# The last four pairs through all experts, and a new cut of the other 28 into chunks

## The chip, the cores and the metric

One core of one Trainium2 chip. The metric is the device time of one execution in microseconds (us), the median of the runs shown.

## The reference

Inputs: `x` (64, 128, 256), a context (64, 128, 192), and weights. Per sequence:

```
x = x + cross_attention(layernorm(x), context)     # 16 heads of 64, 128 queries, 128 keys, then a projection
x = x + experts(layernorm(x))                      # 8 experts, top 2 per token
experts: probs = softmax(t @ gate.T); w, idx = top_k(probs, 2)
         y_e = silu(t @ expert_w[e].T + expert_b[e])          # e = 0..7, 256 -> 256
         out = (sum over the 2 picked of w * y_idx) @ combine_w.T
```

Everything is in float32. The expert biases are eight times as large as drawn.

## The kernel before, in words

**Precision.** Each operand of a matmul is split in a high part (`fp32r`) and the rest, and a product is three matmuls: high by high, high by low, low by high (`three`). ScalarE writes the high part out of PSUM (`split_hi`, L703), VectorE subtracts it for the low one (`split_lo`, L845). SiLU is made of a tanh on ScalarE (L757) and `(1 + tanh) * y` on VectorE (L910); the half is in the routing weights.

**Pairs and slots.** Two sequences (256 tokens) are a pair, 32 in all. A pair's attention takes eight slots, one for two heads; slot `s` belongs to pair `s // 8`, `u = s % 8`. In each slot every engine goes through its own list in program order. TensorE: transpose the probabilities of the slot before, early jobs, queries and keys three slots ahead, scores of the next slot, mid jobs, attend, project, late jobs. GpSimd: split the attended values, divide the probabilities by their sums (`normalise_probs`, L1139, once a slot), then scatters (L1158) and gathers (L1170). SyncE issues the direct transfers, in order, among them the copies `k_s<-qk_s` that each slot's scores wait for.

**Jobs of a slot.** They share three PSUM banks (`gen_ps`). Of the attention: values (slots 1, 2, 5, 6), transposes of the normalised input (3) and of the attention's normalised output (4, `turn_x1`, into `x1T`), gate logits (5), and rank (7): for each token the row that it gets in the table of its expert.

**Experts.** Pairs are gathered in chunks, `CHUNKS = (8, 8, 7, 6, 3)`. Tokens are scattered by expert into `sorted_x` in HBM (four indirect transfers a pair, two pairs later). After the last pair of a chunk VectorE lists its blocks (`list_blocks`, L994 to L1020, in slot 7), and SyncE clears the rows behind each expert's last token (`clear_after`, L370: eight transfers whose addresses are values read from memory). A chunk of `n` pairs has `4n + 7` blocks of 128 rows: 163 in all. A block is one slot: load its rows (L408), its expert's split weights (L422, 512 KB) and bias, two transposes (L617), seven matmuls of 256 columns, tanh, SiLU, store into `sorted_y` (L429). The weights have a ring of three.

**Mixes.** For each pair: four gathers from `sorted_y`, four multiplications by the routing weights on ScalarE (`weigh`, L787), eight transposes that add the two picks (`turn_sum`, L584) in the next slot, split, and `combine`, 12 matmuls, one slot on; VectorE adds the residual (L916) and SyncE stores the output (L483). The chain of one pair goes through one buffer, `mT_s`.

**Order.** `Plan` writes out which slot runs which block (`turn`), gather and mix. `room` gives how many gathers a slot may issue: in the attention 0 in slots 0 to 3 and 1 in slots 4 to 7; behind it 2, and later 4. Attention ends with slot 255. Blocks in slots up to 255: 123 of the 163; mixes up to slot 255: 16 of 32. The rest, 40 blocks and 16 mixes, runs behind the attention; the last slot is 310.

Of the kernel before, what the change touches and what calls it, by code (L numbers as in the profile page):

```python
# [22 lines left out]
CHUNKS = (8, 8, 7, 6, 3)  # L23
# [15 lines left out]
KINDS = ("value", "turn_x", "turn_x1", "gate", "rank", "turn_block", "expert", "turn_mixed", "combine")  # L39
# [11 lines left out]
class Plan:  # L51


    def __init__(self, pairs):
        assert sum(CHUNKS) == pairs
# [7 lines left out]
        for c, end in enumerate(self.ends):  # L63
# [5 lines left out]
            for m in range(end - CHUNKS[c], end):  # L69
# [7 lines left out]
                free += 1  # L77
        self.last = max(max(self.turn) + 4, max(self.mix) + 4)
        self.jobs_at, order = {}, []
        for s in range(-SLOTS, self.last + 1):  # L80
            i, u = s // SLOTS, s % SLOTS
            early, mid, late = [], [], []
            for kind, k, off in ATTENTION_JOBS.get(u, []):
                if 0 <= i + off < pairs:
                    mid.append((kind, (i + off) * per(kind) + k))
# [28 lines left out]
def xattn_moe_kernel(nc, x, ctxT, wq, wkv, wkv_rest, wproj, bproj, gateT, expertT, expert_b, combineT, out):  # L114
# [21 lines left out]
    with ExitStack() as stack:  # L136
# [19 lines left out]
        ones_s = sb("ones_s", [P, P], F32R)  # L156
        minus_half = sb("minus_half", [P, 2])
# [23 lines left out]
        before_f = sb("before_f", [P, P])[:, :]  # L181
# [30 lines left out]
        y_row = carve(4 * max(CHUNKS), 1)  # L212

# [18 lines left out]
        row_f = sb("row_f", [P, pairs, 4])  # L232
# [70 lines left out]
        rstd_done = [sem(f"rstd_done{n}") for n in (1, 2)]  # L303

# [37 lines left out]
        def _(sp):  # L342
# [87 lines left out]

            load_x(0)
# [10 lines left out]
            for s, i, u in slots():  # L442
# [47 lines left out]
        def _(pe):  # L490
# [56 lines left out]
            def project(j, p):  # L547
# [5 lines left out]
                if j == 0 and p == HEAD_PAIRS - 1:  # L553
                    pe.wait_ge(bias_in, 16)
                    pe.wait_ge(const_r, 2)
# [40 lines left out]
            def gate(j, bank):  # L596
# [3 lines left out]
                for t in range(2):  # L600
                    mm = products(bank[:, t * 2 * E:(t + 1) * 2 * E], [
                        (part[:, a, t * P:(t + 1) * P], wgate[:, a, :]) for a in range(2) for part in x1T])
                return mm

            def rank(j, bank):
                pe.wait_ge(hot_done, j + 1)
                if j == 0:
                    pe.wait_ge(const_r, 2)
# [32 lines left out]

            def general(s, position):
                for kind, n in plan.jobs_at[s, position]:
# [19 lines left out]
                    elif kind == "turn_mixed":  # L663
                        pe.wait_ge(weighted, n + 1)
                        mm = turn_sum(got[n % 2], bank)
                    else:
# [4 lines left out]
            for s, i, u in slots():  # L671
# [23 lines left out]
                general(s, "late")  # L695


        @block.scalar
        def _(act):
# [59 lines left out]
            def general(s, position):  # L759
                for kind, n in plan.jobs_at[s, position]:  # L760
# [9 lines left out]
                    elif kind == "turn_x1":  # L770
                        wait(act, made["gate"], n)
                        to = x1T[0][:, :, :].rearrange("p a n -> p (a n)")
                        split_hi(made[kind], n + 1, [(to, bank[:, :])], hi_of[kind])
# [27 lines left out]
            for s, i, u in slots():  # L801
# [11 lines left out]
                if s - 2 in plan.turn:  # L813
                    tanh(plan.turn[s - 2][2])
                general(s, "early")
# [9 lines left out]
                if s in plan.mix:  # L825
# [15 lines left out]
        def _(dve):  # L841
# [101 lines left out]
            def route_top(j):  # L943
# [10 lines left out]
                if j == 0:  # L954
# [4 lines left out]
                                       ALU.is_equal))  # L959
                both = picks.rearrange("p (t k) e -> p t k e", k=2)  # L960
# [11 lines left out]

            def chosen_of(j):
                n = j - (plan.ends[plan.chunk_of[j]] - CHUNKS[plan.chunk_of[j]])
# [47 lines left out]
            def general(s, position):  # L1022
                for kind, n in plan.jobs_at[s, position]:
# [6 lines left out]
                    elif kind in ("turn_x", "turn_x1", "turn_mixed"):  # L1030
                        hi, lo = (y[:, :, :].rearrange("p a n -> p (a n)") for y in
                                  {"turn_x": xT[n % 2], "turn_x1": x1T, "turn_mixed": mT_s}[kind])
                        split_lo(hi_of[kind], n + 1, [(lo, bank[:, :], hi)], drained[kind])
# [22 lines left out]
            for s, i, u in slots():  # L1056
# [7 lines left out]
                if u == 2 and before:  # L1064
                    add_residual(i - 1)
                general(s, "early")
# [25 lines left out]
                if u == 3 and before:  # L1092
                    wait(dve, made["turn_x1"], i - 1)
                    wait(dve, scattered[(i - 1) % 2], 64 * ((i - 1) // 2))
# [7 lines left out]
                if u == 0 and exists(i - 2):  # L1102
                    route_weights(i - 2)
                if i == -1 and u == 4:
# [12 lines left out]
        def _(pool):  # L1117
# [68 lines left out]
            pool.memset(ones_s[:, :].bitcast(F32), 1.0).then_inc(const_r, 1)  # L1186
            pool.memset(before_f, 1.0).then_inc(const_c, 1)
# [5 lines left out]
            for s, i, u in slots():  # L1193
# [11 lines left out]
                if u < 4 and exists(i - 2):  # L1205
# [46 lines left out]
```

## Time and profile before

| | |
|---|---|
| runs | 1726.19 us median of three (1721.33 to 2524.45) |
| the profiled execution | 1724.26 us, span 1722.5 us, mean granted TensorE clock 0.957 |
| busy: TensorE, VectorE, ScalarE, GpSimd | 90%, 72%, 62%, 53% of the span |
| moved by DMA | 303.81 MB, 176 GB/s over the span |

Busy shares are of the span of the profiled execution. In tables of stretches PEclk is the granted clock of TensorE, 1.00 being 2.4 GHz and 0.50 being 1.2 GHz; a value between them is a mean over both levels.

### The profile page before, as it was taken

Reading aid. Unit: us, or ns where it says so; the run is one execution under the profiler, and the core shown is the slowest. Engines: PE = TensorE matmul, PEld = TensorE weight load, DVE = VectorE, ACT = ScalarE, POOL = GpSimd, SP = SyncE. Lnnn points to the kernel's source line nnn. Section 1 sums busy time; section 2 is a strip of 40 time slices with the busy share of each in tenths; the row PEclk is TensorE's granted clock in tenths of the full one; section 3 lists DMA queues with packets and bytes.
Section 4 is the critical chain, followed back from the end, with each engine's and each line's share of the span. In section 5 each row is a group of like instructions: output and inputs, shape, how many; then the busy total and the mean of one; then the engine's idle time right before and its main releaser. Section 6 shows DMA issues by size and latency. Waiting matters only on the chain.

```text
span 1722.5 us, 39484 instructions
## 1 busy us (share of the span) xinstructions
PE 1547.0 (90%) x11835; PEld 1473.5 (86%) x11835; DVE 1236.4 (72%) x3090; ACT 1063.0 (62%) x2904; POOL 915.1 (53%) x1214
## 2 busy tenths in 40 slices
PE   4889999999999999989999999899999989865664
PEld 4789999898999999988999999889999989854554
DVE  6667878887888888877787878877888778642222
ACT  5656666665666766666676666666667656632232
POOL 4645555654555455665555556555555566542132
PEclk9999999999999999999999999999999999977577
DMA  6733333333677775335777775357777645777784
GB/s 226 248 102 93 90 93 99 91 92 102 182 215 219 212 216 156 104 106 165 224 224 223 221 219 150 103 171 223 221 223 226 176 118 171 219 234 234 240 277 149
DMA packets 187211, 303.81 MB, mean 176 GB/s; under 512 B 24725, under 2 KB 119162, under 8 KB 186490
## 3 DMA queue, kind: packets, MB, share of 16 engines
q1 hardware_dynamic: 174714, 267.71, 52.7%
q0 software_dynamic: 12288, 33.57, 5.9%
q8 instruction: 99, 1.62, 0.4%
q14 instruction: 110, 0.90, 0.2%
HBM read 164.06 MB, written 70.01 MB: 136 GB/s over the span
## 4 chain that ended last, share of the span: by engine, by line
PE 61%; DVE 11%; issue 8%; POOL 6%; ACT 5%; SPq 5%; DMA 3%; POOLq 0%; ACTq 0%; DVEq 0%
PE gen_ps L493 18%; PE qk_ps L493 13%; PE proj_ps L493 8%; PE s_ps L493 7%; PE o_ps L493 7%; PE pT_ps L534 5%; POOL sorted_x L1158 1%; PE gen_ps L617 1%; PE gen_ps L584 1%; POOL o_s_lo L1150 1%; ACT v_s_hi L703 1%; DVE stats L861 1%; DVE sums L894 1%; POOL rstd L1134 1%; ACT stage L703 1%
## 5 line engine op out<-in xcount | busy, mean ns | idle before, releaser
L730 ACT ACTIVATE stage<-s_ps,neg_max 128x128 f32<-128x128 f32 x1024 | 293.0, 371 | 126.8 <-DVE neg_max L887 114.4
L1148 POOL CAST o_s_hi<-stage 128x256 fp32r<-128x256 f32 x256 | 102.1, 399 | 474.7 <-ACT stage L703 473.1
L1139 POOL TENSOR_TENSOR stage<-stage,inv_sums 128x512 f32<-128x512 f32 x256 | 266.2, 1040 | 20.5 <-DVE inv_sums L896 20.5
L493 PE MATMUL s_ps<-k_s,qk_s 128*128 128x256 f32 x1536 | 227.4, 284 | 13.9 <-DMA k_s<-qk_s 13.3
L703 ACT CAST pT_s_hi<-pT_ps 128x512 fp32r<-128x512 f32 x256 | 151.0, 590 | 129.2 <-PE pT_ps L534 121.0
L894 DVE TENSOR_REDUCE sums<-stage 128x4 f32<-128x512 f32 x256 | 174.9, 683 | 73.3 <-ACT stage L730 68.5
L493 PEld LDWEIGHTS s_ps<-k_s,qk_s 128*128 128x128 f32 x1536 | 201.5, 191 | 15.5 <-DMA k_s<-qk_s 14.4
L845 DVE TENSOR_TENSOR qk_s<-qk_ps,qk_s 128x512 fp32r<-128x512 f32 x256 | 175.7, 686 | 44.2 <-ACT qk_s L703 43.7
L845 DVE TENSOR_TENSOR pT_s_lo<-pT_ps,pT_s_hi 128x512 fp32r<-128x512 f32 x256 | 172.0, 672 | 46.6 <-ACT pT_s_hi L703 43.8
L1170 POOL DMA_INDIRECT stage<-sorted_y,y_row_of x128 | 126.3, 987 | 141.5 <-issue 68.9
L1150 POOL TENSOR_TENSOR o_s_lo<-stage,o_s_hi 128x256 fp32r<-128x256 f32 x256 | 188.1, 735 | 21.1
L703 ACT COPY stage<-o_ps 64x256 f32<-64x256 f32 x512 | 188.4, 368 | 3.6 <-POOL o_s_lo L1150 0.6
L703 ACT CAST v_s_hi<-gen_ps 128x512 fp32r<-128x512 f32 x128 | 75.1, 587 | 182.6 <-PE gen_ps L493 178.3
L887 DVE TENSOR_REDUCE neg_max<-s_ps 128x4 f32<-128x512 f32 x256 | 174.4, 681 | 10.7 <-PE s_ps L493 10.7
L493 PE MATMUL qk_ps<-xT_hi,wq_s_hi 128*128 128x256 f32 x512 | 166.9, 326 | 15.6 <-DVE wkvr_s_lo L856 9.3
L493 PE MATMUL o_ps<-pT_s_hi,v_s_hi 128*128 128x256 f32 x512 | 156.1, 305 | 24.5 <-DVE pT_s_lo L845 22.7
L845 DVE TENSOR_TENSOR xbT_lo<-gen_ps,xbT_hi 128x256 fp32r<-128x256 f32 x163 | 69.1, 424 | 138.4 <-ACT xbT_hi L703 117.6
L703 ACT CAST qk_s<-qk_ps 128x512 fp32r<-128x512 f32 x256 | 152.4, 595 | 25.0 <-PE qk_ps L493 19.9
L493 PE MATMUL gen_ps<-w_block,xbT_hi 128*128 128x256 f32 x652 | 140.4, 309 | 28.9 <-DMA w_block<-expert_table 12.2
L493 PE MATMUL proj_ps<-wproj_s_hi,o_s_hi 128*128 128x256 f32 x512 | 149.8, 293 | 15.8 <-POOL o_s_lo L1150 15.1
L534 PE MATMUL pT_ps<-ident,stage 128*128 128x128 f32 x1024 | 156.9, 276 | 1.6 <-POOL stage L1139 1.0
L1158 POOL DMA_INDIRECT sorted_x<-xn,row_of x128 | 135.1, 1056 | 23.8 <-issue 23.5
(169 smaller groups left out, 4815.9 us busy)
## 6 DMA issues: line engine op xcount, KB each, us to landing
w_block<-expert_table SPq DMA_DIRECT2D x163, 512.0 KB
k_s<-qk_s SPq DMA_DIRECT2D x512, 128.0 KB
stage<-sorted_x SPq DMA_DIRECT2D x163, 128.0 KB
sorted_y<-stage SPq DMA_DIRECT2D x163, 128.0 KB
x_raw<-in_x SPq DMA_DIRECT2D x32, 256.0 KB
c_raw<-in_ctxT SPq DMA_DIRECT2D x32, 256.0 KB
stage<-in_x SPq DMA_DIRECT2D x32, 256.0 KB
x_kept<-x SPq DMA_DIRECT2D x32, 256.0 KB
```

What stands on the lines that cost most here:

```text
L493: mm = pe.matmul(out_ap, l, r, start=start and n == 0, stop=stop and n == len(terms) - 1, skip_group_check=skip)
L534: mm = pe.transpose(pT_ps[:, k * P:(k + 1) * P], probs[p % 2][:, k, :], ident[:, :])
L703: last = act.copy(to, of)
L730: last = act.activation(probs[p % 2][:, k, :], s_ps[:, k * P:(k + 1) * P], ACT.Exp, bias=neg_max[p % 2][:, k:k + 1])
L845: last = dve.tensor_tensor(lo, of, hi.bitcast(F32), ALU.subtract)
L887: dve.tensor_reduce(neg_max[p % 2][:, :], s_ps[:, :].rearrange("p (k n) -> p k n", k=4), AX_X, ALU.max, negate=True).then_inc(max_done, 1)
L894: dve.tensor_reduce(sums[p % 2][:, :], probs[p % 2][:, :, :], AX_X, ALU.add).then_inc(sums_done, 1)
L1139: pool.tensor_tensor(probs[b][:, :, :], probs[b][:, :, :], inv_sums[b][:, :].unsqueeze(2).broadcast_to([P, 4, P]), ALU.mult).then_inc(prob ...
L1148: pool.tensor_copy(hi[:, :, :], o_full).then_inc(o_hi, 1)
L1150: pool.tensor_tensor(lo[:, :, :], o_full, hi[:, :, :].bitcast(F32), ALU.subtract).then_inc(o_lo, 1)
L1158: pool.indirect_dma_start(out=sorted_x, out_offset=bass.IndirectOffsetOnAxis(ap=row_of[:, j % 4, k:k + 1], axis=0), in_=xn2[j % 2][:, k // ...
L1170: pool.indirect_dma_start(out=got[m % 2][:, k, :], out_offset=None, in_=sorted_y[c], in_offset=bass.IndirectOffsetOnAxis(ap=y_row_of[:, m, ...
```

## The change

Pairs 28 to 31 leave the sorted path. They have no rank, no scatter and no gather. When their gate is done (`dense_weights`), VectorE turns the two picks and weights of each token into eight weights, six of them zero. Behind the attention SyncE loads the split weights of all eight experts (four transfers of 1 MB, pieces of 1 KB) over the attention's own weights `wq_s` and `wkv0_s`, and the biases over `wkvr_s` (`load_all_experts`, issued at slot 254). A dense job is one token tile (128 tokens) by two experts: seven matmuls of 512 columns, a tanh of 512, `(1 + tanh) * y` of 512, and two additions of 256 columns into the tile's sum, each scaled by that expert's weight. Eight jobs a pair, 32 in all, three a slot in slots 258 to 267 and two in slot 268. They use the four PSUM banks of the attention (`s_ps`, `pT_ps`, `o_ps`, `qk_ps`). A dense pair's mix is four transposes of that sum, split, and the same `combine`.

The other 28 pairs are cut `(8, 8, 6, 4, 2)`: 39, 39, 31, 23 and 15 blocks, 147 in all. Up to slot 255 there are 143 blocks and 23 mixes; four blocks and nine mixes come behind. The lists and clears of all five chunks fall in the attention (before: four). `room` now gives two gathers in slots 4 to 7, so that up to two pairs are mixed in eight slots, in slots 7 and 1. The last slot is 280.

Small moves: `row_f` and `before_f` go into other buffers, and a constant `first_two` (ones in two rows) takes the place of `ones_s` beside the bias of all experts.

```diff
-CHUNKS = (8, 8, 7, 6, 3)
+CHUNKS = (8, 8, 6, 4, 2)
+SPARSE = sum(CHUNKS)
+DENSE_JOBS = 8
+DENSE_BANKS = 4
+DENSE_PER_SLOT = 3
...
+        self.dense = {}
+        at = SLOTS * pairs + 2
+        for n in range(DENSE_JOBS * (pairs - SPARSE)):
+            m = SPARSE + n // DENSE_JOBS
+            if n % DENSE_JOBS == 0:
+                at = max(at, SLOTS * (m + 2))
+            while len(self.dense.get(at, [])) >= DENSE_PER_SLOT:
+                at += 1
+            self.dense.setdefault(at, []).append(n)
+            if n % DENSE_JOBS == DENSE_JOBS - 1:
+                self.mix[max(at + 2, max(self.mix) + 2)] = m
...
-            return 0 if u < 4 else 1
-        return 4 if i > pairs + 1 else 2
+            return 0 if u < 4 else 2
+        return 4 if s >= SLOTS * pairs + 2 else 2
...
+            def load_all_experts():
+                sp.wait_ge(qk_made, pairs * HEAD_PAIRS)
+                sp.wait_ge(made["value"], 4 * pairs)
+                rows = expert_table[0:E * P, :].rearrange("(e p) c -> p e c", p=P)
+                for part in range(2):
+                    for a in range(2):
+                        to = w_all[part][a].bitcast(F32).rearrange("p (e c) -> p e c", e=E)
+                        at = (2 * part + a) * C
+                        sp.dma_start(to, rows[:, :, at:at + C]).then_inc(dense_in, 16)
+                sp.dma_start(b_all[0:2, :].bitcast(F32).rearrange("h (e c) -> h e c", e=E),
+                             bias_table[0:2 * E, :].rearrange("(e h) c -> h e c", h=2)).then_inc(dense_in, 16)
...
+                if s == SLOTS * pairs - 2:
+                    load_all_experts()
...
+            def dense(n):
+                m, t, q = SPARSE + n // DENSE_JOBS, n % DENSE_JOBS // 4, n % 4
...
+                wait(pe, drained["dense"], n - DENSE_BANKS + 1)
+                pe.wait_ge(drained["turn_x1"], m + 1)
+                cols, rows = slice(q * 2 * C, (q + 1) * 2 * C), slice(t * P, (t + 1) * P)
+                terms = []
+                for a in range(2):
+                    terms += three(xT1[m], (w_all[0][a], w_all[1][a]), lambda y: y[:, a, rows], lambda w: w[:, cols])
+                terms.append((first_two[:, :], b_all[:, cols]))
+                products(dense_ps[n % DENSE_BANKS][:, :], terms).then_inc(made["dense"], 1)
...
+            def tanh_all(n):
+                act.wait_ge(made["dense"], n + 1)
+                wait(act, drained["dense"], n - 1)
+                act.activation(th_all[n % 2], dense_ps[n % DENSE_BANKS][:, :], ACT.Tanh, scale=0.5).then_inc(dense_tanh, 1)
...
+            def dense_out(n):
+                dve.wait_ge(dense_tanh, n + 1)
+                wait(dve, dense_added, 2 * (n - 1))
+                dve.scalar_tensor_tensor(out=y_all[n % 2], in0=th_all[n % 2], scalar=1.0,
+                                         in1=dense_ps[n % DENSE_BANKS][:, :],
+                                         op0=ALU.add, op1=ALU.mult).then_inc(drained["dense"], 1)
...
+            def dense_add(n):
+                m, t, q = n // DENSE_JOBS, n % DENSE_JOBS // 4, n % 4
+                dve.wait_ge(drained["dense"], n + 1)
...
+                for h in range(2):
+                    to = acc[m][:, t, :]
+                    y, w = y_all[n % 2][:, h * C:(h + 1) * C], dense_w[:, m, t, 2 * q + h:2 * q + h + 1]
+                    if q + h == 0:
+                        ins = dve.tensor_scalar(to, y, w, None, ALU.mult)
+                    else:
+                        dve.wait_ge(dense_added, 2 * n + h)
+                        ins = dve.scalar_tensor_tensor(out=to, in0=y, scalar=w, in1=to, op0=ALU.mult, op1=ALU.add)
+                    ins.then_inc(dense_added, 1)
```

## Rows read from the trace of the kernel before

**Rows 1.** Stretches (us from the start): busy time and count by engine, PEclk, DMA share, GB/s

```profile
287.20:328.00 40.80, 39.22 (x304) 37.15 (x304) 32.75 (x81) 27.62 (x75) 23.95 (x34) 1.00 0.35 92
504.50:551.00 46.50, 46.45 (x379) 45.35 (x378) 38.14 (x97) 32.20 (x91) 23.97 (x34) 1.00 0.73 216
922.60:972.30 49.70, 49.05 (x399) 47.60 (x398) 39.34 (x99) 34.09 (x96) 28.14 (x39) 1.00 0.75 224
...
1560.00:1686.00 126.00, 78.97 (x431) 69.36 (x431) 34.84 (x76) 39.08 (x100) 27.60 (x29) 0.72 0.84 257
...
1703.00:1708.00 5.00, 3.45 (x17) 3.08 (x15) 0.69 (x1) 2.29 (x5) 3.03 (x4) 0.50 0.30 85
```

**Rows 2.** Timeline of GpSimd, slot 0 of pairs 6, 7, 11, 12, 20, 21; slot 255

```profile
287.22 1.04 POOL L1139 TENSOR_TENSOR stage<-stage,inv_sums 128x512 f32<-128x512 f32 x1
...
328.01 1.04 POOL L1139 TENSOR_TENSOR stage<-stage,inv_sums 128x512 f32<-128x512 f32 x1
...
504.52 1.04 POOL L1139 TENSOR_TENSOR stage<-stage,inv_sums 128x512 f32<-128x512 f32 x1
...
551.02 1.04 POOL L1139 TENSOR_TENSOR stage<-stage,inv_sums 128x512 f32<-128x512 f32 x1
...
922.61 1.04 POOL L1139 TENSOR_TENSOR stage<-stage,inv_sums 128x512 f32<-128x512 f32 x1
...
972.26 1.04 POOL L1139 TENSOR_TENSOR stage<-stage,inv_sums 128x512 f32<-128x512 f32 x1
...
1498.59 1.04 POOL L1139 TENSOR_TENSOR stage<-stage,inv_sums 128x512 f32<-128x512 f32 x1
```

**Rows 3.** The page's part on DMA issues: count, KB each, us to landing

```profile
w_block<-expert_table SPq DMA_DIRECT2D x163, 512.0 KB
...
sorted_x<-zero_rows SPq DMA_DIRECT2D x1, 4992.0 KB, 17.1
```

**Rows 4.** Timeline of GpSimd: slots 7 and 1 without and with list and clear

```profile
323.42 1.04 POOL L1139 TENSOR_TENSOR stage<-stage,inv_sums 128x512 f32<-128x512 f32 x1
...
332.34 1.03 POOL L1139 TENSOR_TENSOR stage<-stage,inv_sums 128x512 f32<-128x512 f32 x1
...
405.36 1.04 POOL L1139 TENSOR_TENSOR stage<-stage,inv_sums 128x512 f32<-128x512 f32 x1
...
419.43 1.04 POOL L1139 TENSOR_TENSOR stage<-stage,inv_sums 128x512 f32<-128x512 f32 x1
```

**Rows 5.** Timeline of SyncE: the clear behind the attention; the store of slot 254

```profile
1547.45 10.93 SPq L370 DMA_DIRECT2D sorted_x<-zero_rows  x8
...
1493.49 0.34 SPq L429 DMA_DIRECT2D sorted_y<-stage  x1
```

**Rows 6.** Timeline of GpSimd, slot 255: what it waits for after a gather

```profile
1497.42 0.40 POOL L1148 CAST o_s_hi<-stage 128x256 fp32r<-128x256 f32 x1 [1.50 <-ACT stage L703]
```

**Rows 7.** Timeline of TensorE: 512 columns at either clock, and a mix's transposes

```profile
555.65 0.40 PE L493 MATMUL gen_ps<-wkv_s_hi,cT_lo 128*128 128x512 f32 x1
555.89 0.40 PE L493 MATMUL gen_ps<-wkv_s_lo,cT_hi 128*128 128x512 f32 x1
...
92.30 0.63 PE L493 MATMUL gen_ps<-wkv_s_hi,cT_lo 128*128 128x512 f32 x1
92.73 0.63 PE L493 MATMUL gen_ps<-wkv_s_lo,cT_hi 128*128 128x512 f32 x1
...
1521.07 1.10 PE L584 MATMUL gen_ps<-ident,stage 128*128 128x128 f32 x8
```

**Rows 8.** Groups by line and shape, 1500 to 1722 us: busy, mean ns, idle before

```profile
L910 DVE SCALAR_TENSOR_TENSOR stage<-stage,gen_ps 128x256 f32<-128x256 f32 x42 | 17.4, 415 | 18.5 <-DMA sorted_y<-stage 17.9 <-issue 0.3 <-ACT stage L757 0.3
...
L916 DVE TENSOR_TENSOR stage<-gen_ps,stage 128x512 f32<-128x512 f32 x16 | 11.0, 685 | 7.9 <-PE gen_ps L493 7.9
L703 ACT CAST mT_s_hi<-gen_ps 128x512 fp32r<-128x512 f32 x16 | 9.4, 587 | 37.9 <-PE gen_ps L584 34.9 <-issue 3.0
```

**Rows 9.** Timeline of VectorE: the last instruction

```profile
1718.82 0.69 DVE L916 TENSOR_TENSOR stage<-gen_ps,stage 128x512 f32<-128x512 f32 x1 [3.02 <-PE gen_ps L493]
```

More of the change, by code:

```diff
@@ L38 @@
 }
-KINDS = ("value", "turn_x", "turn_x1", "gate", "rank", "turn_block", "expert", "turn_mixed", "combine")
+KINDS = ("value", "turn_x", "turn_x1", "gate", "rank", "turn_block", "expert", "turn_mixed", "combine", "dense")
 def per(kind):
@@ L83, in __init__ @@
             for kind, k, off in ATTENTION_JOBS.get(u, []):
-                if 0 <= i + off < pairs:
+                if 0 <= i + off < (SPARSE if kind == "rank" else pairs):
                     mid.append((kind, (i + off) * per(kind) + k))
@@ L212, in xattn_moe_kernel @@
         y_row = carve(4 * max(CHUNKS), 1)
+        row_f = carve(4, pairs)
+        w_all = [[wq_s[part][:, :, :].rearrange("p a n -> p (a n)"), wkv0_s[part][:, :]] for part in range(2)]
+        b_all = wkvr_s[0]
+        over_v = [v_s[part][:, 0, 0:2 * N2].rearrange("p (a n) -> p a n", a=2) for part in range(2)]
+        whole = lambda pair: [y[:, :, :] for y in pair]
+        xT1 = {j: whole(x1T) for j in range(pairs)}
+        xT1.update({pairs - 3: whole(xT[(pairs - 2) % 2]), pairs - 2: whole(xT[(pairs - 1) % 2]), pairs - 1: over_v})
+        th_all = [y.rearrange("p k n -> p (k n)") for y in probs]
+        y_all = [y[:, :, :].rearrange("p t n -> p (t n)") for y in (x_raw, c_raw)]
+        acc = [xn2[SPARSE % 2][:, :, :], xn2[(SPARSE + 1) % 2][:, :, :], xb, x1[:, :, :]]
+        dense_picks = sb("dense_picks", [P, pairs - SPARSE, 4, E])
+        dense_w = sb("dense_w", [P, pairs - SPARSE, 2, E])
         stats = [sb(f"stats{n}", [P, 2, 6]) for n in (1, 2)]
@@ L303, in xattn_moe_kernel @@
         rstd_done = [sem(f"rstd_done{n}") for n in (1, 2)]
+        two_zero = sem("two_zero")
+        dense_in, dense_tanh, dense_added, dense_w_done = (
+            sem(n) for n in ("dense_in", "dense_tanh", "dense_added", "dense_w_done"))
+        dense_ps = [s_ps, pT_ps, o_ps, qk_ps]
         block = stack.enter_context(nc.Block())
@@ L601, in gate @@
                     mm = products(bank[:, t * 2 * E:(t + 1) * 2 * E], [
-                        (part[:, a, t * P:(t + 1) * P], wgate[:, a, :]) for a in range(2) for part in x1T])
+                        (part[:, a, t * P:(t + 1) * P], wgate[:, a, :]) for a in range(2) for part in xT1[j]])
                 return mm
@@ L695, in _ @@
                 general(s, "late")
+                for n in plan.dense.get(s, []):
+                    dense(n)
         @block.scalar
@@ L814, in _ @@
                     tanh(plan.turn[s - 2][2])
+                for n in plan.dense.get(s - 1, []):
+                    tanh_all(n)
                 general(s, "early")
@@ L824, in _ @@
                 general(s, "mid")
-                if s in plan.mix:
+                if plan.mix.get(s, SPARSE) < SPARSE:
                     weigh(plan.mix[s])
@@ L1030, in general @@
                     elif kind in ("turn_x", "turn_x1", "turn_mixed"):
-                        hi, lo = (y[:, :, :].rearrange("p a n -> p (a n)") for y in
-                                  {"turn_x": xT[n % 2], "turn_x1": x1T, "turn_mixed": mT_s}[kind])
-                        split_lo(hi_of[kind], n + 1, [(lo, bank[:, :], hi)], drained[kind])
+                        hi, lo = {"turn_x": xT[n % 2], "turn_x1": xT1.get(n), "turn_mixed": mT_s}[kind]
+                        split_lo(hi_of[kind], n + 1, [(lo[:, :, :], bank[:, :].rearrange("p (a n) -> p a n", a=2), hi[:, :, :])],
+                                 drained[kind])
                     elif kind == "turn_block":
@@ L1065, in _ @@
                     add_residual(i - 1)
+                todo = plan.dense.get(s - 1, [])
+                for k, n in enumerate(todo):
+                    dense_out(n)
+                    if k > 0:
+                        dense_add(n - 1)
+                if todo:
+                    dense_add(todo[-1])
                 general(s, "early")
```

60 lines of the change are left out of this document (50 added, 10 removed).

## The prediction

> **What bounds the kernel now.** I read the table of stretches first [rows 1]. In the attention TensorE is busy for 39.2 of 40.8 us in a pair without blocks, 46.45 of 46.5 with eight blocks, and 49.05 of 49.7 with eight blocks and a mix: there it has next to nothing left, and each block or mix moved in is paid. Behind the attention the reader should see another bound: from 1560 to 1686 us TensorE is busy for 79 of 126 us at a granted clock of 0.72, while the DMA engines are at 0.84 and 257 GB/s. A block brings 512 KB of weights [rows 3], so the tail is paced by transfers.
>
> Then the timeline of GpSimd, where `normalise_probs` marks every slot [rows 2]. The attention ends at 1498.6 us; the span ends at 1722.5. The tail is **224 us** for 40 blocks and 16 mixes. That is what the change attacks.
>
> **Attention: what is moved in.** Pair 6 (no blocks) takes 328.01 - 287.22 = 40.8 us, pair 11 (eight blocks) 46.5, pair 20 (eight blocks, a mix) 49.65 [rows 2]. So a block costs 5.7 / 8 = 0.71 us there and a mix 3.15.
> - 20 more blocks up to slot 255 (143 for 123): 14.3 us.
> - 7 more mixes (23 for 16): 22.0 us. TensorE alone has some 2.4 us in one: eight transposes (1.1) and 12 matmuls of 256 columns at half of the 0.235 us of one of 512 [rows 7]. That is the lower end for a mix. The changed plan puts two of them into slots 7 and 1 of eight; no pair of before does that, so the price of the second is the unknown: between 2.4 us and twice 3.15.
> - One more list and clear. From slot 7 to slot 1 takes 419.43 - 405.36 = 14.1 us with them and 332.34 - 323.42 = 8.9 without [rows 4]: 5.2 us. Two of the clears (slots 216 and 232) now fall where blocks run; they hold SyncE for 10.9 us behind the attention [rows 5], but in the attention weights are issued about two slots, some 12 us, before they are used.
> - The second gather of a slot: GpSimd still idled 1.50 us in slot 255 behind one gather and ahead of the next attended values [rows 6], and a gather is about 1.0 us, 1.2 with its gap. It fits; were it not to, I would pay 0.3 us a slot in 80 slots at most, 24 us. In block slots, which are longer, it has more room. I take 0.
> - Removed: the rank of three pairs and the scatters of two. They lie beside TensorE's work; 0 to 3 us.
>
> The sum is 41.5. Four of the early mixes now run in slots without blocks, where TensorE is not full, and the mix of slot 255 does its work behind the attention. I take **+38 us** (range 30 to 65), so slot 255 comes at 1536.6.
>
> **Tail, start of the dense jobs.** The store of slot 254 was issued 5.1 us before slot 255's mark [rows 5, 2], and the big load follows it. For its time the nearest row is the transfer of 4992 KB in pieces of 1 KB, 17.1 us [rows 3]; 4.1 MB by that is 14 us. With a block's weights in front, it lands about 11 us behind the mark. The weights of the last blocks are issued after it on the same queue, and TensorE wants blocks 143 and 144 before the first dense job. I take 15 us from the mark to the first dense job; 10 to 28 are possible.
>
> **Tail, the dense slots 258 to 268.** TensorE's sum at 2.4 GHz:
> - 32 jobs of seven matmuls, 0.235 us each [rows 7]: 52.6 us.
> - four mixes: 4 x (1.0 + 1.4) = 9.5; three experts and two block transposes: 3.0; `turn_x1` and gate of pair 31: 1.5.
> Together 66.6 us. VectorE's sum: a dense job is one operation of 512 columns (0.685) and two of 256 (0.415 each, and some 0.05 for waiting on its own semaphore) [rows 8], 1.6 us; 32 of them are 51.5. Add 5.5 for the mixes, 2.5 for blocks, 5 for the last pair's normalisation and top 2: 64.5 us. ScalarE has a tanh of 512 (about 0.59, as its cast of 512) a job, 19 us in all. So two engines are nearly full together, with four banks and two buffers between them. I add 3 us for friction: **70 us**.
>
> **Tail, the end.** Mixes 27 to 31 come behind the last dense job and go one by one through `mT_s`: transposes 0.5, high part 0.59, low part 0.69, combine 1.4, handovers 0.25: 3.4 us at 2.4 GHz. At 1.2 GHz a matmul of 512 columns starts every 0.43 us in place of 0.235 [rows 7], which gives 5.1. The end of before ran at either level, 0.50 from 1703 to 1708 us [rows 1]. I take 4.4 x 5 = 22 us, and 3.7 from the last addition to the end of the span (1722.5 - 1718.8) [rows 9]: **26 us**.
>
> The tail is 15 + 70 + 26 = 111 us where it was 224. The span: 1536.6 + 111 = 1647.6; with the 1.8 us that the profiled execution had beside its span, **1649 us**. Against its 1724.26 that is 75 us less, 4.4%. The median of the runs lies 1.9 us above that execution, so nothing is to be corrected.
>
> **The rivals.**
> *A. The dense slots run at 1.2 GHz.* TensorE fell to the lower level in the tail whenever it waited for transfers [rows 1], and here it waits for a load of 4 MB first, then hands every job over to two engines. Price: 32 x 7 x (0.43 - 0.235) = 43.7 us, and some 12 for mixes and blocks: 1705 us, 1.1% faster, no change to speak of. Against it: the jobs are queued densely, 1.6 us each, with four banks ahead, and the attention, which hands over as often, ran at 1.00. Chance 0.12.
> This is where the Trainium skill speaks against the change. Its page "TensorE: Matmul & The Clock Gate", section "A second HAM failure mode: psum-queue depth-cycling", tells of a kernel with matmuls of 512 columns that cycles through PSUM banks and whose engine idled so often between groups that its clock went up and down. By that rule the time would be up to the one of rival A. The trace's attention also cycles through banks and doesn't show it.
>
> *B. VectorE's chain sets the dense slots.* Each addition waits for the one before it, and a job's result for tanh. Were a job to take 2.4 us on that chain, the dense slots would take 25 us more: 1674 us. For it: the two sums are within 3% of each other. Against it: the order puts the next job's product between a job's own steps. Chance 0.10.
>
> *C. Two mixes in eight slots hinder each other in the attention.* If each mix cost twice 3.15 us, that is 22 x 3.15 = 69 us more, 1718 us, no change. Against it: TensorE has 2.4 us of work in one. Chance 0.05.
>
> *D. The dense slots go one job at a time: slower.* If the next job's matmuls start only when the sum of the one before is there, a job takes 7 x 0.43 (the engine would idle, and so be at its lower level), 0.59, 0.685, 0.83 and 0.3 for handovers: 5.4 us, 173 us for 32 in place of 53. That is 1649 + 120 = 1769 us, slower by 2.6%; it is slower than the bound from 5.2 us a job on. Against it: four banks, and buffers for two jobs of tanh and product. Chance 0.03.
>
> *E. The load holds up the blocks behind it.* If the four last blocks each wait for their weights behind 4 MB, the dense jobs start at 30 us, 15 later: 1664 us. For it: before, copies of the attention were late behind the transfer of 4992 KB. Chance 0.10, inside the forecast's range.
>
> **How the numbers follow.** The forecast, 1649 us with 1625 to 1672, has 0.60. The low end is the attention at +30 and the tail at 95; the high end has the load late and a dense job of 1.9 us. B and E hold 0.20, A 0.12, C 0.05, D 0.03. The range of 1622 to 1700 leaves out D, C, half of A and the luck beyond 1622: less than 2 in 10. A change of under 2% can't be told from none; the bound lies at 1691.7 us, so faster has 0.83 (forecast, B, E, and the mild half of A that stays below the bound at 0.03), same 0.14, slower 0.03.
>
> **What would show it.** Slot 255's mark at 1530 to 1545 us; pairs 24 to 30 of 52 to 56 us; a first dense matmul some 15 us later; 32 groups of seven dense matmuls, starting 0.235 us apart, in 65 to 75 us at a granted clock near 1.00, with VectorE busy for nine tenths; a DMA share that falls to little behind the load; GpSimd idle, and no idle time ahead of the attended values that a gather ends. The prediction is wrong if the dense stretch shows PEclk near 0.5, if pairs with two mixes take over 60 us, or if TensorE waits for `dense_in` or block weights for over 15 us.

## The result, and the profile after

The changed kernel takes **1665.37 us**, median of four (1662.45 to 1667.21); the kernel before took 1724.74, median of four beside it. The ratio is **0.9658 [0.9643, 0.9672]**: 3.4% faster. One of the four runs of the kernel before took 2524.45 us, a slow one, which the ratio leaves out. Forecast were 1649 us, in a range of 1622 to 1700. The profiled execution had 1667.21 us and a span of 1665.4.

The page of the changed kernel, its slices and its largest group of transfers. In the slices each digit stands for a fortieth of the span: the busy share, for PEclk the granted clock, in tenths.

```profile
span 1665.4 us, 39339 instructions
PE 1548.1 (93%) x11891; PEld 1475.1 (89%) x11891; DVE 1269.0 (76%) x3134; ACT 1060.3 (64%) x2888; POOL 880.6 (53%) x1184
...
PE   4989999998999999999999999999999998999696
...
PEclk9989999999999999999999999999999999999898
DMA  6743333333577777344677677467776776877621
...
w_block<-expert_table SPq DMA_DIRECT2D x147, 512.0 KB
```

The DMA row now falls to 2 and 1 at the end, where before a stretch of 126 us ran at 0.84 [rows 1], and `w_block` has 147 transfers for 163 [rows 3].

The timeline of GpSimd, `normalise_probs` of slots 192, 200, 218, 219 and 255:

```profile
1118.03 1.04 POOL L1276 TENSOR_TENSOR stage<-stage,inv_sums 128x512 f32<-128x512 f32 x1
1171.95 1.04 POOL L1276 TENSOR_TENSOR stage<-stage,inv_sums 128x512 f32<-128x512 f32 x1
...
1296.03 1.03 POOL L1276 TENSOR_TENSOR stage<-stage,inv_sums 128x512 f32<-128x512 f32 x1
1306.91 1.04 POOL L1276 TENSOR_TENSOR stage<-stage,inv_sums 128x512 f32<-128x512 f32 x1
...
1540.23 1.04 POOL L1276 TENSOR_TENSOR stage<-stage,inv_sums 128x512 f32<-128x512 f32 x1
```

Slot 255 comes at 1540.2, 41.6 us later than before [rows 2], and the tail is 125.2 us instead of 224. Stretches of the changed kernel, columns as in [rows 1]:

```profile
1118.00:1172.00 54.00, 52.53 (x424) 50.69 (x423) 40.90 (x101) 36.23 (x101) 31.94 (x43) 1.00 0.76 224
...
1540.00:1550.00 10.00, 6.25 (x47) 5.50 (x46) 3.10 (x10) 5.30 (x15) 7.54 (x11) 0.95 1.09 351
1550.00:1560.00 10.00, 6.31 (x31) 6.10 (x31) 1.54 (x3) 2.36 (x6) 1.80 (x2) 0.54 1.02 364
1560.00:1570.00 10.00, 7.87 (x45) 6.70 (x45) 6.30 (x15) 4.34 (x10) 3.97 (x6) 1.00 0.53 183
1570.00:1580.00 10.00, 7.74 (x33) 6.69 (x34) 4.02 (x10) 2.12 (x5) 0.80 (x1) 0.83 0.13 40
1580.00:1590.00 10.00, 6.69 (x28) 5.78 (x27) 5.58 (x12) 2.07 (x4) 0.00 (x0) 0.66 0.20 66
1590.00:1600.00 10.00, 10.00 (x56) 8.59 (x55) 6.08 (x14) 4.59 (x9) 0.46 (x1) 1.00 0.04 15
...
1620.00:1630.00 10.00, 10.00 (x50) 8.29 (x49) 9.36 (x20) 5.33 (x11) 0.00 (x0) 1.00 0.09 28
1640.00:1650.00 10.00, 5.87 (x26) 5.53 (x27) 3.68 (x7) 0.58 (x1) 0.00 (x0) 0.55 0.26 87
```

Four phases are to be seen: transfers at full load until 1560; a bad start of the dense work until 1590 (TensorE busy for 6.7 to 7.9 of 10 us, clock 0.66 to 1.00); then TensorE full at 1.00 until 1630 (also in the two stretches not shown); and the last mixes. A DMA share above 1 is read as full. The timeline of TensorE, in the order of its waits, says what ended them:

```profile
1553.62 0.66 PE L667 MATMUL gen_ps<-ident,stage 128*128 128x128 f32 x2 [6.58 <-DMA stage<-sorted_x]
...
1563.10 0.40 PE L543 MATMUL s_ps<-wq_s_hi,x1T_hi 128*128 128x512 f32 x1
...
1572.26 0.39 PE L543 MATMUL gen_ps<-wcomb_s_hi,mT_s_hi 128*128 128x256 f32 x1 [3.05 <-DVE stage L996]
...
1584.06 1.97 PE L634 MATMUL gen_ps<-ident,stage 128*128 128x128 f32 x8 [3.31 <-DVE stage L996]
...
1642.59 0.55 PE L543 MATMUL gen_ps<-wcomb_s_hi,mT_s_hi 128*128 128x256 f32 x1 [3.85 <-DVE mT_s_lo L931]
```

The first wait is for the rows of a block. The queue of SyncE shows why they are late:

```profile
1534.90 0.39 SPq L475 DMA_DIRECT2D wq_s_hi<-expert_table  x1
1535.33 0.97 SPq L475 DMA_DIRECT2D wkv_s_hi<-expert_table  x1
1536.34 2.21 SPq L475 DMA_DIRECT2D wq_s_lo<-expert_table  x1
1538.59 3.01 SPq L475 DMA_DIRECT2D wkv_s_lo<-expert_table  x1
1541.64 3.46 SPq L476 DMA_DIRECT2D wkvr_s_hi<-bias_table  x1
1546.13 0.36 SPq L444 DMA_DIRECT2D stage<-sorted_x  x1
```

The five issues of the load hold SyncE for 10.2 us, and the block's rows (128 KB) are issued 11.2 us after the first MB, behind all 4 MB. TensorE could start on them 7.5 us after their issue. The next two waits are for line 996, the product that ends a block and frees one of the three general banks. VectorE's timeline shows where it stands in that engine's order:

```profile
1568.83 0.69 DVE L1073 SCALAR_TENSOR_TENSOR x_raw<-stage,o_ps 128x512 f32<-128x512 f32 x1 [0.16 <-ACT stage L865]
1569.44 1.00 DVE L1096 SCALAR_TENSOR_TENSOR xn<-c_raw,dense_w,xn 128x256 f32<-128x256 f32 x2
1570.54 1.00 DVE L1096 SCALAR_TENSOR_TENSOR xn<-x_raw,dense_w,xn 128x256 f32<-128x256 f32 x2
1571.46 0.42 DVE L931 TENSOR_TENSOR xbT_lo<-gen_ps,xbT_hi 128x256 fp32r<-128x256 f32 x1
1571.79 0.41 DVE L996 SCALAR_TENSOR_TENSOR stage<-stage,gen_ps 128x256 f32<-128x256 f32 x1
...
1662.05 0.69 DVE L1002 TENSOR_TENSOR stage<-gen_ps,stage 128x512 f32<-128x512 f32 x1 [1.83 <-PE gen_ps L543]
```

`dense_out` and `dense_add` of a slot's three jobs come first, the block's work behind them. TensorE's `combine` at 1572.26 needs that bank, so it waits until the slot's three products and six additions are through (the last product and the last four additions are above), and the next dense jobs, which stand behind the combine in TensorE's order, wait with it.

Set against the forecast, in us of the profiled execution:

| | forecast | measured | |
|---|---|---|---|
| slot 255's mark | 1536.6 | 1540.2 | +3.6 |
| mark to first dense matmul (1563.1) | 15 | 22.9 | +7.9 |
| dense matmuls (to the end of the last, 1637.9) | 70 | 74.8 | +4.8 |
| from there to the end of the span | 26 | 27.5 | +1.5 |
| span | 1647.6 | 1665.4 | +17.8 |

### The profile page after: what moved, and what is told of

It reads as the page before. It is cut to its first block, busy times and chain, and to the rows that moved or that the text cites. A ratio compares the mean times of both kernels' runs of the same rounds, so it can differ in the third digit from the quotient of the medians.

```text
span 1665.4 us, 39339 instructions
## 1 busy us (share of the span) xinstructions
PE 1548.1 (93%) x11891; PEld 1475.1 (89%) x11891; DVE 1269.0 (76%) x3134; ACT 1060.3 (64%) x2888; POOL 880.6 (53%) x1184
## 4 chain that ended last, share of the span: by engine, by line
PE 63%; DVE 12%; issue 8%; ACT 6%; POOL 5%; SPq 3%; DMA 3%; ACTq 0%; DVEq 0%; POOLq 0%
PE gen_ps L543 19%; PE qk_ps L543 13%; PE proj_ps L543 8%; PE s_ps L543 7%; PE o_ps L543 7%; PE pT_ps L584 5%; ACT stage L776 2%; DMA k_s<-qk_s 2%; POOL sorted_x L1295 1%; PE gen_ps L634 1%; ACT v_s_hi L776 1%; PE gen_ps L667 1%; DVE stats L947 1%; POOL o_s_lo L1287 1%; DVE neg_max L973 1%
## 5 line engine op out<-in xcount | busy, mean ns | idle before, releaser
L543 PE MATMUL s_ps<-k_s,qk_s 128*128 128x256 f32 x1536 | 227.5, 284 | 18.1 <-DMA k_s<-qk_s 17.8
L543 PE MATMUL o_ps<-pT_s_hi,v_s_hi 128*128 128x256 f32 x512 | 156.2, 305 | 22.9 <-DVE pT_s_lo L931 20.4
L776 ACT CAST qk_s<-qk_ps 128x512 fp32r<-128x512 f32 x256 | 152.9, 597 | 22.0 <-PE qk_ps L543 16.6
L543 PE MATMUL o_ps<-pT_s_lo,v_s_hi 128*128 128x256 f32 x512 | 145.0, 283 | 0.0
L543 PE MATMUL o_ps<-pT_s_hi,v_s_lo 128*128 128x256 f32 x512 | 144.9, 283 | 0.0
L543 PE MATMUL qk_ps<-xT_lo,wq_s_hi 128*128 128x256 f32 x512 | 144.1, 281 | 0.0
L543 PE MATMUL proj_ps<-wproj_s_hi,o_s_lo 128*128 128x256 f32 x512 | 143.9, 281 | 0.0
```

The source lines that it names most:

```text
L543: mm = pe.matmul(out_ap, l, r, start=start and n == 0, stop=stop and n == len(terms) - 1, skip_group_check=skip)
L776: last = act.copy(to, of)
```

## The experiments

Ratios are to the kernel before on the same chip. Experiments 1 to 4 ran on one chip (its median there 1713.53 us), 5, 6 and 9 on a second (1723.17), 7, 8 and 10 on a third (1726.3); times of different chips are therefore not subtracted from each other. The changed kernel's 0.9658 stands beside all of them. It ran again on the second chip, to show how well a ratio repeats: 1662.9 us, **0.9652 [0.9638, 0.9665]**, mark of slot 255 at 1537.9, the same waits at the start of the tail.

> The changed kernel itself, to compare the others of this call on the same chip: ratio to the kernel before 0.964 to 0.968.

Up to slot 254 six of these kernels are the same program, and still slot 255's mark lies between 1531.9 and 1542.0 in them. Much of that lies in a few slots behind a list and a clear: slot 218 took 10.0 to 12.5 us in the six, slot 234 took 9.1 to 12.8. A difference between two such marks is therefore rough by several us; smaller effects are read inside a stretch or from the ratio.

**1. One gather a slot in the changed kernel.**

```diff
-            return 0 if u < 4 else 2
+            return 0 if u < 4 else 1
```

> The changed kernel with one gather a slot in slots 4 to 7, as before: 16 mixes up to slot 255 in place of 23, last slot 291 in place of 280. My theory: the tail is now filled by TensorE and VectorE, so a mix costs there as much as in the attention. Attention about 25 us shorter (mark of slot 255 near 1515 us), tail 25 to 35 us longer: 1665 to 1677 us, ratio to the kernel before 0.965 to 0.972. Rival 1, the second gather is what made the attention's slots long (over the mixes' own work): 1650 us or less. Rival 2, the second gather is what pays for the change: over 1685 us.

Measured: 1678.94 us, 0.9797 [0.978, 0.9813]. The theory's 0.965 to 0.972 failed. By the time alone rival 2 (over 1685 us) is not reached, but that bound was set beside 1724.7 us, where it is a ratio of 0.977, and the ratio lies above it. The mark came at 1528.6 and the tail was 148.3 us. Experiments 3 and 4 ran on the same chip with two gathers in the attention: marks at 1535.4 and 1531.9, tails of 122.2 and 121.2. Of the waits of TensorE behind the attention of this kernel (total, times, longest), the largest:

```profile
PE gen_ps L543 <- DVE mT_s_lo L931: 16.1, 11, 1.6
```

So two gathers are worth 1.4% here, some 24 us, more than I expected. Seven mixes more behind the attention made the tail 26 to 27 us longer, 3.8 us a mix: there each goes through `mT_s` and pays the handovers. What they cost in the attention the marks leave between 3.4 and 6.9 us. Without the 25 slots that differ by over 0.5 us among the six kernels with one program up to slot 254, it is 12 us, 1.7 us a mix; the single execution here was slow in slots of a list or clear (slot 186 took 10.5 us where the others took 6.6 to 7.9, slot 234 took 13.9), and that makes up most of the difference. The 1.7 is a mean of two prices. In pairs 16 and 17, with no block and two, where TensorE is busy for 41.1 of 45.7 and 44.8 of 47.5 us here, the further mix costs 1.2 us each (46.9 and 48.7 us in the changed kernel). In pairs 24 and 25, with eight blocks and TensorE busy for 49.0 of 49.7 and 49.6 us, it costs 4.2 and 3.7 us (53.9 and 53.3), about what it costs behind the attention.

**2. Two gathers a slot in the kernel before.**

```diff
-            return 0 if u < 4 else 1
+            return 0 if u < 4 else 2
```

> The kernel before with nothing changed but two gathers a slot in slots 4 to 7: 20 mixes up to slot 255 in place of 16. The old tail is paced by transfers of weights, and mixes hide there. My theory: attention 13 to 15 us longer, tail shorter only by what the last gathers had to wait, 0 to 10 us: 1727 to 1740 us, ratio 1.002 to 1.009. Rival: the tail gets shorter by as much as the attention gets longer or more, ratio 0.99 to 1.00.

Measured: 1708.4 us, 0.9973 [0.9951, 0.9995]. The theory, 1.002 to 1.009, failed; the rival's range holds. The mark came at 1503.0, the tail was 206 us. The 1498.6 and 224 us of the kernel before are of a chip on which it took some 11 us longer, so the 18 us between the tails are not all the gathers' doing; the ratio says 0.3% for both effects together. TensorE's longest waits in that tail are still for weights and rows of blocks and for line 910 behind them. The two parts of the change help each other: alone, gathers give 0.3% and dense pairs with new chunks 2.0%, together 3.4%. The dense pairs and the new chunks were not run apart.

**3. The load of the expert weights, one MB a slot**, the biases behind the last. In the loop of SyncE:

```diff
-                if s == SLOTS * pairs - 2:
-                    load_all_experts()
+                if SLOTS * pairs - 2 <= s < SLOTS * pairs + 2:
+                    load_all_experts(s - SLOTS * pairs + 2)
```

> The changed kernel with the four 1 MB transfers of all experts issued one a slot in slots 254 to 257, between the blocks' own loads, in place of all at slot 254; the same bytes. Theory: TensorE's 6.6 us wait for a block's rows and its time at 1.2 GHz behind it come from queueing behind 4 MB. First dense matmul 17 us or less behind slot 255's mark in place of 22.9; 1656 to 1661 us, ratio 0.960 to 0.963. Rival 1: the last piece lands later and the dense jobs wait for that as long: 1664 to 1667 us. Rival 2: the time before the dense jobs isn't on the path, since VectorE sets the dense slots: no change either, but with the first dense matmul earlier.

Measured: 1657.53 us, 0.966 [0.9639, 0.9681]: no gain, and the theory's 0.960 to 0.963 failed. The wait for the block's rows was gone. The first dense matmul came 20.2 us behind the mark instead of 22.9 (21.7 in the second run of the changed kernel), not the 17 expected, and there were two new waits: 2.17 us for the biases (under experiment 7), and before it 2.52 us for GpSimd's last `o_s_lo`. That one stands behind two gathers in GpSimd's order, the second after an idle stretch:

```profile
1542.76 0.94 POOL L1309 DMA_INDIRECT stage<-sorted_y,y_row_of  x1 [1.25 <-issue]
```

**4. Short additions.** In 24 of 32 jobs the second addition takes 8 columns, not 256; the rest of that expert's share is left out of the output.

```diff
+                        some = slice(0, C if h == 0 or q == 0 else 8)
-                        ins = dve.scalar_tensor_tensor(out=to, in0=y, scalar=w, in1=to, op0=ALU.mult, op1=ALU.add)
+                        ins = dve.scalar_tensor_tensor(out=to[:, some], in0=y[:, some], scalar=w, in1=to[:, some],
+                                                       op0=ALU.mult, op1=ALU.add)
```

> The changed kernel, but the second addition of each dense job (24 of the 32) adds 8 columns in place of 256; it leaves out the rest of every second expert's share, except for one in four. VectorE has some 0.3 us less work a job, 7 to 8 us in all, TensorE the same. If VectorE sets the dense slots: 5 to 8 us less, ratio 0.961 to 0.963. If TensorE does: 0 to 1 us in the dense slots, and 2 to 4 us of the wait of the first combine behind them (VectorE ended 4 us behind TensorE there): ratio 0.964 to 0.966.

Measured: 1654.67 us, 0.9651 [0.9635, 0.9667]: the case in which TensorE sets the dense slots. The dense stretch took 73.5 us instead of 74.8, the end 25.2 instead of 27.5. Each shortened addition took 0.226 us instead of 0.483, so VectorE had 24 x 0.257 = 6.2 us less to do, and the dense stretch moved by 1.3. Rival B, VectorE's chain as the bound, falls.

**5. The clears, two a slot.** `clear_after` issues two of its eight transfers in each of slots 0 to 3 of the pair.

```diff
-                if u == 0 and i - 1 in plan.ends:
-                    clear_after(plan.ends.index(i - 1))
+                if u < 4 and i - 1 in plan.ends:
+                    clear_after(plan.ends.index(i - 1), u)
```

> The changed kernel with the eight clears behind each chunk issued two a slot in slots 0 to 3, in place of eight in slot 0. Theory: the eight of them hold SyncE for 8 to 11 us, the key copies behind them come late, and the attention pays it five times (most where blocks run, slots 218 and 234: intervals of 10.9 and 12.3 us for 8.6). Mark of slot 255 at 1526 to 1532 us in place of 1540.2; 8 to 14 us less in all, ratio some 0.959. Rival: what makes these slots long is VectorE's list of blocks in slot 7, which stays: 0 to 3 us less.

Measured: 1657.92 us, 0.9613 [0.9595, 0.963], some 7 us less: under the 8 to 14 expected, above the rival's 3. Slot 218 took 8.60 us; in the changed kernel it took 10.88 (1296.03 to 1306.91, above). There the eight clears stood in front of everything else on SyncE, among it the copies of the keys, and TensorE waited for such a copy in slot 218. First SyncE of the changed kernel:

```profile
1280.36 8.03 SPq L406 DMA_DIRECT2D sorted_x<-zero_rows  x8
...
1292.05 1.15 SPq L398 DMA_DIRECT2D k_s<-qk_s  x2
...
1297.89 1.16 SPq L398 DMA_DIRECT2D k_s<-qk_s  x2
```

then its TensorE:

```profile
1297.88 0.98 PE L543 MATMUL s_ps<-k_s,qk_s 128*128 128x256 f32 x6 [2.93 <-DMA k_s<-qk_s]
```

and GpSimd with the clears spread (8.60 us between the marks; slot 234 took 8.60 too, where it had taken 12.26):

```profile
1291.66 1.03 POOL L1277 TENSOR_TENSOR stage<-stage,inv_sums 128x512 f32<-128x512 f32 x1
1300.26 1.03 POOL L1277 TENSOR_TENSOR stage<-stage,inv_sums 128x512 f32<-128x512 f32 x1
```

**6. Blocks and mixes ahead of the dense work** in the orders of VectorE and ScalarE; nothing else moves. VectorE's part (ScalarE's puts `general(s, "early")` ahead of `tanh_all`):

```diff
-                todo = plan.dense.get(s - 1, [])
-...
                 general(s, "early")
                 if s - 2 in plan.turn:
                     expert_out(plan.turn[s - 2][2])
                 if s - 3 in plan.mix:
                     combined(plan.mix[s - 3])
+                todo = plan.dense.get(s - 1, [])
+...
```

> The changed kernel with the order inside a slot turned on VectorE and ScalarE: the split of a block, the block's SiLU and a mix's last addition stand ahead of the dense jobs' product and additions, not behind them. Theory: TensorE's two waits of 3.0 and 3.3 us for VectorE L996 in the dense slots 259 to 262 are for a bank whose reader stands behind three dense jobs; they fall below 1 us each and the clock stays at 2.4 GHz: 5 to 8 us less, ratio 0.961 to 0.963. Rival: VectorE's sum sets these slots, and the same wait comes back at the dense banks: 0 to 2 us less.

Measured: 1652.92 us, 0.9598 [0.9582, 0.9615], some 10 us less than the changed kernel on the same chip, above what I expected. The dense stretch took 63.8 us instead of 74.8. Stretches of this kernel, whose dense matmuls start at 1560.7:

```profile
1560.00:1570.00 10.00, 9.53 (x56) 8.13 (x55) 4.98 (x13) 4.42 (x10) 4.78 (x6) 1.00 0.52 162
1570.00:1580.00 10.00, 10.00 (x55) 8.54 (x54) 9.50 (x22) 4.74 (x10) 0.00 (x0) 1.00 0.22 66
```

and VectorE's order, in which line 996 now stands ahead of the products of line 1073:

```profile
1566.82 0.41 DVE L996 SCALAR_TENSOR_TENSOR stage<-stage,gen_ps 128x256 f32<-128x256 f32 x1
1567.14 0.68 DVE L1073 SCALAR_TENSOR_TENSOR x_raw<-stage,s_ps 128x512 f32<-128x512 f32 x1
1567.74 0.68 DVE L1073 SCALAR_TENSOR_TENSOR c_raw<-stage,pT_ps 128x512 f32<-128x512 f32 x1
```

TensorE's wait for line 996 at the combine, 3.05 us before, is now 0.47, and the one of 3.31 is gone. TensorE is full at 1.00 from the second stretch on; in the changed kernel that took until 1590. This order, not a lack of engine time, cost the 11.0 us. VectorE's and ScalarE's orders were turned together; line 996 is VectorE's.

**7. The biases ahead of the first MB**, on top of experiment 3.

```diff
+                if k == 0:
+                    sp.dma_start(b_all...)          # issued behind the last MB before
```

> The load of the expert weights is spread over slots 254 to 257 as in load_spread, and the transfer of the biases is issued ahead of the first MB instead of behind the last. In load_spread the first dense job waited 2.17 us for that transfer, whose issue alone took 3.10 us. Theory: the biases are the last thing that the first dense job waits for, so the wait disappears and the first dense job starts some 2 us earlier behind slot 255's mark (18 us instead of 20.2), span 1655 to 1656, ratio 0.963 to 0.966. Rival: the start is paced by the chain of slots 256 and 257 (blocks, the last pair's projection, GpSimd's o_s_lo), and the wait for the biases only lay beside another that now ends last; or the long issue of the biases ahead of slot 255's copies delays the mark by 3 us: ratio 0.966 to 0.968 as load_spread or above.

Measured: 1667.95 us, 0.9657 [0.9635, 0.9679]. The ratio can't tell theory (0.963 to 0.966) from rival (0.966 to 0.968); the start does. The theory wanted it 18 us behind the mark, and it came no earlier than in experiment 3, by a wait that neither had named. The first dense matmul, with the load spread:

```profile
1555.66 0.51 PE L545 MATMUL s_ps<-wq_s_hi,x1T_hi 128*128 128x512 f32 x1 [2.17 <-DMA wkvr_s_hi<-bias_table]
```

and with the biases first as well:

```profile
1562.95 0.50 PE L544 MATMUL s_ps<-wq_s_hi,x1T_hi 128*128 128x512 f32 x1 [4.38 <-DMA wkv_s_lo<-expert_table]
```

It starts 20.9 us behind its mark (1542.0). The fourth MB had been issued at 1552.4 and landed 10.5 us later. Whatever comes last of the load ends the wait, and the DMA engines were at a share of 0.99 to 1.07 in the last 20 us before the start in experiment 3 (1540 to 1560: 1.07 and 0.99) and at 1.04 and 1.07 from 1540 to 1560 here. I read the start as set by 4 MB and the blocks' weights getting through, not by one transfer's place. That is argued from these shares; no run loaded fewer bytes, and in both runs the last MB was also issued late, 9.6 and 10.4 us behind the mark, where it was issued 1.6 us ahead of it before.

**8. The clearing of the spare rows, one block a slot.** In slot 8 SyncE clears the 39 blocks behind the tables (4992 KB, [rows 3]) in one transfer; here 39 transfers go out in slots 8 to 46.

```diff
-                if i == 1 and u == 0:
+                if SLOTS <= s < SLOTS + 39:
...
-                    sp.dma_start(sorted_x[E * REGION:E * REGION + max(plan.blocks) * P, :]...
+                    sp.dma_start(sorted_x[b:b + P, :], zero_rows[:, :]).then_inc(dump_cleared, 16)
```

> The changed kernel with only the clearing of the 39 blocks of dump rows (4992 KB in one transfer in slot 8) cut in 39 transfers of 128 KB, one a slot in slots 8 to 46. Theory: the attention copies queued behind the 4992 KB are late once, which shows as one slot interval of over 16 us where neighbours take 4.4 to 5; spread, that interval falls to 5 and everything behind comes 11 to 12 us earlier, ratio 0.958 to 0.960. Rival: 39 more issues on SyncE and DMA traffic beside the block-free slots cost 0.1 to 0.3 us a slot, and only 4 to 8 us come off: 0.961 to 0.963.

Measured: 1654.98 us, 0.9574 [0.9551, 0.9597], 0.8% or some 14 us less than the changed kernel by the ratios. Marks of slots 10 and 11 in the changed kernel, then here:

```profile
82.83 1.04 POOL L1276 TENSOR_TENSOR stage<-stage,inv_sums 128x512 f32<-128x512 f32 x1
99.40 1.04 POOL L1276 TENSOR_TENSOR stage<-stage,inv_sums 128x512 f32<-128x512 f32 x1
```

```profile
83.69 1.04 POOL L1277 TENSOR_TENSOR stage<-stage,inv_sums 128x512 f32<-128x512 f32 x1
88.91 1.04 POOL L1277 TENSOR_TENSOR stage<-stage,inv_sums 128x512 f32<-128x512 f32 x1
```

The interval falls from 16.6 to 5.2 us, 11.4 of the 14; the rest is within the ratios' own intervals. The kernel before has the 16.6 too; it is no part of the change, but the same mistake as the load: a big transfer ahead of copies that are due.

**9. All together:** experiments 3, 5, 6 and 8.

> The changed kernel with all of it: load of all experts over four slots, clears two a slot, VectorE's order turned, and the clearing of 39 blocks at slot 8 (4992 KB, behind which TensorE waited 9.4 us) one block a slot in slots 8 to 46. If the parts add up: 3 + 10 + 6 + 12 us less than the changed kernel, 1630 to 1638 us against 1665, ratio 0.946 to 0.950 to the kernel before. If they hide one another: 0.953 to 0.958.

Measured: **1635.88 us, 0.949 [0.9477, 0.9503]**, span 1637.4, slot 255 at 1523.7: faster than both kernels, and as the parts added up.

**10. The same with the biases first.**

> As combined (load spread, clears spread, clearing of the dump rows spread, blocks and mixes ahead of the dense work on VectorE and ScalarE), with the biases' transfer ahead of the first MB of weights. In combined the first scores of the dense jobs' stretch waited 3.9 us for the biases. Theory: 2 to 4 us come off: ratio 0.946 to 0.948 where combined had 0.949. Rival: another wait of the same length takes its place: 0.949 or above.

Measured: 1639.03 us, 0.9479 [0.9456, 0.9502]. The wait for the biases (3.90 us) became one of 5.12 us for the last MB; no difference can be told from 0.949.

## Why the prediction was right, and where it was off

The sign and the mechanism were right. A tail paced by the transfers of 40 blocks became one paced by TensorE; the blocks and mixes that moved forward cost in the attention about what was said; 59 of the 75 us came. The prediction's raw sum for the attention, 41.5 us, meets the measured 41.6 partly by luck: the mark differs by up to 10 us between executions of one program.

**Blocks and mixes in the attention** held: eight blocks without a mix take 46.5 us as before, with two mixes 53.0 to 53.9 (pairs 18, 24, 25, 30). Against 49.65 with one [rows 2] the second mix costs 3.4 to 4.3 us, inside 2.4 to 6.3. Of pairs 24 to 30, which the prediction saw at 52 to 56 us, three lay outside: pair 28 with one mix at 49.1, pairs 27 and 29 at 56.2 and 57.9, the two with slots 218 and 234. Rival C had 2 x 3.15 for every mix, and falls.

**The clears** failed. "in the attention weights are issued about two slots, some 12 us, before they are used" looked at one user of SyncE's queue; the key copies of each slot stand in it too, with less lead. Slots 218 and 234 became 2.3 and 3.7 us longer (1.4 to 3.9 and 0.5 to 4.2 in the six kernels with this program), and experiment 5 gives 7 us back in all.

**The second gather** ("It fits", and "I take 0") held in the attention, with little to spare. In slot 255 GpSimd was idle for 0.28 us behind two gathers, where it had been 1.50 behind one [rows 6], and the wait ended with ScalarE, not with a gather:

```profile
1539.07 0.40 POOL L1285 CAST o_s_hi<-stage 128x256 fp32r<-128x256 f32 x1 [0.28 <-ACT stage L776]
```

The 2.52 us for GpSimd in experiment 3 stand in slot 256, which has two gathers in the kernel before too. That the second gather is worth 24 us of the gain (experiment 1) the prediction had in its seven mixes but did not single out.

**The start of the dense jobs** is the largest error: 15 us taken, 22.9 measured. The load was taken to land 11 us behind the mark; the DMA engines ran at full share until about 1560, some 20 us behind it, with the blocks' transfers in between. Rival E named that mechanism and gave it 30 us. Half of its delay came: the wait of 6.58 us for one block's rows. But experiments 3 and 7 showed that the wait itself isn't the price: taken away, two others of 2.2 to 4.4 us took its place in each, and the ratio stayed. The price is, as far as the shares say, the traffic, at a DMA share of 1.02 to 1.09. What would start the dense jobs earlier is a load that ends before slot 255, and that needs room other than the attention's own weights. That was not tried.

**The dense slots**: "I add 3 us for friction" failed in kind. The sum of TensorE's work, 66.6 us, was above what is needed (63.8 in experiment 6), and matmuls of 512 columns did start 0.23 us apart. The other 11.0 us were two waits of 3.05 and 3.31 us for line 996 and, by the rows' durations, some 4 us of work at the half clock behind them (the eight transposes at 1584.06 took 1.97 us, those at 1561.33 1.09). The prediction counted the engines' loads and the four banks of the dense jobs, and missed that blocks and mixes share a different set of three banks whose readers stand last in VectorE's order.

**Rival A** appeared in the dense slots only there: 0.83 and 0.66 from 1570 to 1590, each time behind a wait of over 3 us, then 1.00 for as long as TensorE was full. The section "A second HAM failure mode: psum-queue depth-cycling" of the Trainium skill's page "TensorE: Matmul & The Clock Gate" ties such a swing of the clock to frequent short idle times between groups in a kernel that cycles through banks. No such idle times stand here: from 1590 to 1630 the same four banks are cycled through with TensorE busy throughout, and the clock is 1.00. The cycling alone did not lower it.

**Rival B** falls by experiment 4. An addition did take 483 ns, where the prediction had 415 and some 50 for a wait, and VectorE was busy for 9.0 to 9.4 of 10 us in the stretches from 1600 to 1630, so it is close to the bound. **Rival D** did not occur: jobs overlap, at 1.6 us each.

**The end** was 1.5 us too short. Forecast were 22 us for five mixes, and from the last dense matmul to the last addition it was 24.2; the first mix waited 3.85 us for the work of VectorE that had piled up. The 4.4 us a mix held: the periods between the five were 5.3, 5.2, 3.6 and 3.6 us, two at the half clock and two at the full, 4.4 in the mean.

## What to carry to other kernels

Where engines go through written orders, work that gives back a shared bank stands ahead of work that only feeds its own chain: here that alone was worth 10 us, and neither busy shares nor a sum of work showed it. A further mix cost 1.2 us in pairs where TensorE had 2.7 to 4.6 us to spare, and about 4, as much as behind the attention, where it had less than 1. Before a long transfer or a row of issues is put into a queue, list everything that passes the same queue in the next ten microseconds with its due time; cut into pieces of one slot's size, two such transfers gave 14 and 7 us. A big load that ends the wait for the next stage was, as these traces read, priced by the traffic up to its last byte, and moving its parts about only changed the name of the wait.

## What the runs showed of the hardware that was not expected

- SyncE's issue time of one and the same transfer (1 MB in pieces of 1 KB) grew from 0.39 to 0.97, 2.21 and 3.01 us when four were issued in a row; spread over slots each took 0.39 to 0.60. The small transfer of biases (16 KB) took 3.46 us behind all four (1.11 to 3.00 in the other runs with this order), 2.48 to 3.10 right behind one, and 0.28 to 0.29 ahead of it.
- `scalar_tensor_tensor` of 256 columns with both tensors in SBUF and a scalar for each partition took 483 ns (L1096), with one tensor in PSUM and a number as the scalar 415 ns before and 410 after (L910, L996); which of the two differences makes it was not tried. With 8 columns the first form took 226 ns (experiment 4), so 248 further columns cost 257 ns.
- The DMA engines moved 364 GB/s for 10 us here (1550 to 1560), and up to 377 in experiment 7. In the tail of before the mean was 257 [rows 1], and its busiest 10 us (1640 to 1650) had 300.
